# SAGE rounds of a graph network: GpSimd waits for the landing of two gathers in place of a clear between packets of two

## The reference, cut to what matters

```
def _sage_conv(x, src, dst, W_l, b_l, W_r, n_nodes):      # rounds 0 and 1
    agg = segment_sum(x[src], dst)                        # x[src]: the gather of this case
    mean = agg / maximum(cnt, 1.0)[:, None]
    out = mean @ W_l + b_l + x @ W_r
    return out / maximum(norm(out), 1e-12)
h = relu(_sage_conv(x, ...)); h = relu(_sage_conv(h, ...)); x = layernorm(x + h)

def sage_conv(h, W_l, W_r, bias):                         # rounds 2 to 5
    agg = segment_sum(h[src], dst) * inv_deg[:, None]
    return relu(agg @ W_l + h @ W_r + bias)
x = layernorm(x + h)                                      # after round 5
```

## Time and profile before

| | us |
|---|---|
| median of 3 runs | 14431.09 |
| lowest, highest | 14413.74, 14431.66 |
| the profiled execution's own time | 14447.17 |
| its span, first to last instruction | 14445.4 |
| PE busy | 9623.8 (67%) |
| DVE busy | 8218.2 (57%) |
| GpSimd busy | 5322.8 (37%) |
| ACT busy | 4574.6 (32%) |

### The profile page before, as it was taken

The page is one execution under the profiler, slowest core; times in us unless marked ns, Lnnn a source line. Parts: engine busy times, 40 slices in busy tenths (PEclk is TensorE's granted clock), DMA queues, the critical chain, the costliest instruction groups (busy, mean ns, idle before and its releaser), DMA issues. The chain is left out here.

```text
span 14445.4 us, 272192 instructions
## 1 busy us (share of the span) xinstructions
PE 9623.8 (67%) x51477; PEld 7110.9 (49%) x51673; DVE 8218.2 (57%) x25011; ACT 4574.6 (32%) x9542; POOL 5322.8 (37%) x6651
## 2 busy tenths in 40 slices
PE   2765567766666777777787777544544477777765
PEld 1112157755555666666666666333333244444444
DVE  4776567767774222222223555688888644444467
ACT  0000012235553222222222444455555422222257
POOL 0554543322222333333333333333333255555510
PEclk9887778877888988888988888666666678787776
DMA  9300046655555665665665666433333333333368
GB/s 324 116 3 1 1 136 195 194 160 180 181 180 165 186 186 180 186 184 176 184 188 175 208 209 210 137 123 122 116 122 122 114 95 98 99 98 94 96 193 270
DMA packets 2090713, 2169.75 MB, mean 150 GB/s; under 512 B 312033, under 2 KB 1419234, under 8 KB 2077614
## 3 DMA queue, kind: packets, MB, share of 16 engines
q1 hardware_dynamic: 1343046, 1025.71, 23.7%
q10 hardware_dynamic: 584524, 871.96, 17.5%
q0 software_dynamic: 163072, 271.31, 7.5%
HBM read 1407.48 MB, written 826.93 MB: 155 GB/s over the span
## 5 line engine op out<-in xcount | busy, mean ns | idle before, releaser
L778 POOL DMA_INDIRECT gath<-node_a,g_idx x1176 | 1130.4, 961 | 2606.5 <-PE edge_bank L980 1825.4
L1120 PE MATMUL o_bank<-keep,gsrc_t 128*128 (+1 forms) x9408 | 1475.6, 307 | 841.4 <-DMA keep<-rank_rows 810.3
L1844 DVE TENSOR_TENSOR gsrc_t<-node_no,keep 128x512 f32<-128x512 f32 x1176 | 807.9, 693 | 2125.9 <-PE o_bank L1120 1567.6
L1120 PEld LDWEIGHTS o_bank<-keep,gsrc_t 128*128 128x128 f32 x9408 | 1328.3, 218 | 958.4 <-issue 956.7
L1108 PE MATMUL o_bank<-w_r,h_t 128*128 128x128 f32 x9408 | 1744.2, 342 | 0.0
L1108 PEld LDWEIGHTS o_bank<-w_r,h_t 128*128 128x128 f32 x9408 | 1477.0, 239 | 340.5 <-issue 340.5
L787 POOL DMA_INDIRECT agg<-y_rows,s_idx x784 | 867.4, 1106 | 1445.5 <-DVE s_idx L1811 1082.1
L778 POOL DMA_INDIRECT gath<-node_x,g_idx x784 | 782.4, 998 | 1572.4 <-PE edge_bank L1032 589.5
L778 POOL DMA_INDIRECT gath<-node_b,g_idx x784 | 800.1, 1020 | 1016.4 <-PE edge_bank L980 461.2
L753 POOL DMA_INDIRECT rec_dram<-rec_rows,place_idx x784 | 761.1, 971 | 1093.8 <-DVE rec_rows L1760 857.3
L1295 ACT ACTIVATE h_t<-ht_bank 128x512 f32<-128x512 f32 x1176 | 688.3, 594 | 1345.3 <-PE ht_bank L1098 933.7
(11 more groups left out here) (388 smaller groups left out, 19355.0 us busy)
## 6 DMA issues: line engine op xcount, KB each, us to landing
keep<-rank_rows SPq DMA_DIRECT2D x4704, 64.0 KB
node_a<-h_out ACTq DMA_DIRECT2D x784, 256.0 KB
rank_rows<-y_rows SPq DMA_DIRECT2D x588, 256.0 KB
h_in<-node_a SPq DMA_DIRECT2D x396, 256.0 KB
node_x<-h_out ACTq DMA_DIRECT2D x394, 256.0 KB
node_b<-h_out ACTq DMA_DIRECT2D x394, 256.0 KB
agg<-zeros ACTq DMA_DIRECT2D x98, 1024.0 KB
agg_in<-agg SPq DMA_DIRECT2D x392, 256.0 KB
```

Of the source, the lines that this page charges most:

```text
L778: pool.indirect_dma_start(gath[q][:, k, :], None, h_of, bass.IndirectOffsetOnAxis(g_idx[q][:, k:k + 1], 0)).then_inc(gathered[q], 16)
L1120: last = pe.matmul(o_bank[s][:, j * P:(j + 1) * P], hot_node[s][:, j, :], ranks_at(s, u, j), start=False, stop=j == RPP - 1, skip_group_ch ...
L1844: dve.tensor_tensor(hot_node[s], node_no[:].unsqueeze(1).to_broadcast([P, RPP, P]), of.unsqueeze(2).to_broadcast([P, RPP, P]), ALU.is_equa ...
```

## The change

In the SAGE rounds, behind each two gathers, GpSimd waits until `gathered[q]` shows that these two have landed: the target less 32 behind the first two of a block, the full target behind the last two. The clears and the waits for them go from these rounds, and `pauses` no longer counts them. The first two blocks of a round, and the GAT and TR rounds, stay as they are.

```
-            GATHER_PAUSES = 4 * (PAIRS - 1)
...
-                pauses += GATHER_PAUSES if kind == SAGE else PAUSES
+                pauses += PAUSES if kind in STAGGERED else 0
...
-                def gathers_by_two(q, n, first, r=r):
+                def gathers_by_two(q, n, r=r):
                     pool.wait_ge(gt_ready[q], gt_ready.at(r, n - 1))
                     pool.wait_ge(gidx_ready[q], gidx_ready.at(r, n))
                     pool.sem_inc(pool_turn, 1)
                     for half in range(2):
                         gathers(q, of=range(2 * half, 2 * half + 2))
-                        pause(first + half)
+                        pool.wait_ge(gathered[q], gathered.at(r, n) - 32 * (1 - half))
                         pool.sem_inc(pool_turn, 1)
...
-                    gathers_by_two(q, 2, first_pause + 2 * q)
+                    gathers_by_two(q, 2)
...
-                        gathers_by_two(q, i + 3, i * 4 + (first_pause + 4 + 2 * q))
+                        gathers_by_two(q, i + 3)
```

## The result

The changed kernel takes 14530.91 us (median of 4 runs, 14520.95 to 14533.52) where the kernel before takes 14422.42 (median of 4 runs, 14407.16 to 14431.66). The ratio is 1.0075, with an interval of 1.0058 to 1.0092: 108 us slower. The forecast was 14605, the range 14480 to 14930.

What follows compares the result with a forecast made beforehand. SP's chain of landings was taken to bound rounds 2 to 4, the gather loop the heads. Terms of +84, +30, +45, +5 and +10 sum to +174 us: 14621 profiled, 14605 on the median, range 14480 to 14930.

Steps and rivals of the forecast that it cites:

- heads, 12 pairs: First two throttled pairs of six rounds: gather loop 20.0 us against 13.0, nothing covers it, +84 us.
- round 0: Its 45 middle pairs: loop of 22.0 us against a period of 21.66, plus uneven pairs, +30 us.
- short pairs and middles of rounds 2 to 4: Short pairs behind the heads +5 us a round; middles, loop just under the period, +10 each.
- rounds 1 and 5: Middles with 29.19 and 25.04 us a pair: longer loop hidden, but for some 5 us.
- scatter, ends of rounds: Gathers that now and then take longer than 0.95 us, and scattered landings: +10 us.
- L: Time from the end of the second gather instruction to its landing as seen: 2.0 us in heads, 2.5 in middles.
- B: Length of a pair's gather loop on GpSimd, 12 + 4L: 20.0 us in heads, 22.0 in middles.
- The long landing: Rival: landings of 3.0 us in the middles make the loop 24.0 us and the bound, about +440 us; chance 0.25.
- SP's chain: Rounds 2 to 4: SP's rank loads, their landing and row writes set the period, 22.36 us in one pair.
- uneven pairs and uneven landings use that up at times: +10 each: Middles of rounds 2 to 4: up to 4 us of cover for late turns is sometimes used up, +30 us together.
- Faster transfers on SP's chain: Rival: fewer gathers in flight speed rank loads in rounds 2 to 4; 14355 us at 1.2 a pair; chance 0.09.
- Hidden anyway: Rival: landings of 1.6 to 1.9 us throughout and 0.5 us a pair gained, 14431 give or take 25; chance 0.06.

Runs made afterwards that it cites:

- e2: Changed kernel with landing waits only in the first two throttled pairs of each SAGE round, clears from there on: 14460.83 us against 14369.61 for the kernel before.
- e1: Changed kernel with the clears kept in the first two throttled pairs of each SAGE round, landing waits behind them: 14451.13 us against 14369.61 for the kernel before.
- e6: Kernel before with a 128x2048 clear instead of 128x8 in every SAGE pause, no landing waited for: 14580.75 us against 14469.89.
- e4: Kernel before with landing waits in the middles of rounds 2 to 5 alone, clears in rounds 0, 1 and all heads: 14344.33 us against 14369.61.
- e3: Kernel before with neither clears nor landing waits in the SAGE rounds, eight gathers in a row: 15866.57 us against 14369.61.
- e10: Kernel before with a short clear and wait after each gather in place of each two in the SAGE rounds: 14343.43 us against 14451.64.
- e7: Kernel before with one short clear and wait after each four gathers in place of each two: 15648.92 us against 14469.89.
- e8: Changed kernel with one landing wait after each four gathers in place of each two: 15032.45 us against 14469.89 for the kernel before.
- e12: Kernel before with short clears after each gather in SAGE middles, each gather and scatter in GAT, each two in TR: 14086.84 us against 14479.32.

## Why the prediction was right, and where its sum was not

The direction and the range held, and so did the mechanism in its main part: the gather loop gets longer, it is the path in the heads, and it becomes the bound of rounds 2 to 4 at about their old period. The sum is 66 us too high, term by term:

| term | forecast | trace |
|---|---|---|
| heads, 12 pairs | +84 | +70.6 |
| round 0 | +30 | +47.7 |
| short pairs and middles of rounds 2 to 4 | +45 | -16.5 |
| rounds 1 and 5 | +5 | +37.5 and -25.4 |
| scatter, ends of rounds | +10 | -5.4 |
| sum | +174 | +108.5 |

The heads are the one large term that came out by its own mechanism. Behind them the forecast has +90 and the trace +37.9, which is +85.2 in rounds 0 and 1 less 47.3 elsewhere: that the rest lies near the forecast at all is owed to terms with opposite signs and not to the sum's working.

**Heads.** The step was right and L mis-sized: 1.5 to 1.7 us for most of the gaps where 2.0 was taken, so a head pair is 18.6 to 19.6 us and not 20.0. e2 has the same price with nothing else changed: the heads +75, the SAGE part +73, the time +91. But e1 shows that the heads' price isn't simply added: with the heads cured the middles took most of it back. Whether middles really run longer behind a short head, and why, wasn't found.

**L in the middle.** 2.5 was taken and 2.1 to 2.5 measured (gaps of 2.9 to 3.3 us), so that B is 22.14 us in round 2 where the forecast had 22.0. The eighth gather of a middle pair ends 17.7 to 19.2 us after the first starts (the means of the six rounds), nearly as said. The long landing, the rival with a chance of 0.25, isn't there: no round sits at 24 us except for those that had more before. Two of its numbers don't follow from their rows. The loads in the head added 0.92 to 1.09 us to a landing (2.69 against 1.77 and 1.60), not 0.69, which is the distance from the chosen 2.0. And 3.32 bounded one landing, not all: the longest gap of a middle, 5.7 us, leaves 4.9.

The Trainium skill, "DMA: Bandwidth & Descriptors", section "Anatomy of one DMA — SWDGE (gpsimd) path", has 2.0 us fixed and the bytes over 436 GB/s, an estimate of 2.15 us for such a gather. The traces lie on both sides of it, 1.53 in a quiet head pair and up to 2.5 on average in the middles, so it is a fair first figure but not one to set a 1% decision by. Counted from the start of a gather instruction, which takes 0.95 us itself, the landing comes after 2.5 us or so even in a quiet head. The HBM latency at high load that the Trainium skill gives on the same page, section "Latency and other measured facts", 2 us where the average is 0.2, would have made 3.4 by the prediction's estimate, and no round's mean comes near that.

**Round 0.** The sign is right and the mechanism holds in part: the loop of 22.0 was to pass a period of 21.66, and the pairs became 22.72. PE waits before its turn for 26.4 us where it was 4.5, mostly for gathers. But only 19 of the 45 pairs follow GpSimd's own last work, so the loop isn't the bound of the other 26, and what makes them longer wasn't found. The +30 counted uneven pairs on top of the loop; +47.7 was measured, and +54.8 in e1. e6 is no confirmation: its loop is too short to be the bound and DVE has 97 us more to do.

**Rounds 2 to 4.** The prediction left SP's chain as the bound, with the loop just under it; PE's waits show that the loop took its place (354 us of waits for gathers in rounds 2 and 3, where the earlier trace rows have 394.9 for rank rows). So "uneven pairs and uneven landings use that up at times: +10 each" has the path wrong: the loop replaced SP's chain, at 22.14 to 22.25 us, instead of lying beside it and adding to it at times, and the landings' scatter is in its mean already. The short pairs did grow, from 16.5 to 22.6 us in round 2, but in the changed kernel it was paid back behind them. The sizes say less than the path. These three middles are 16.5 us shorter in the changed kernel, but 24.0 and 19.2 longer in e1 and e4, which have the same landing waits there, and kernels that left them as they were differ by 40 us.

**Rounds 1 and 5.** "Hidden, but for some 5 us" is the step that failed, in both, with opposite signs. The cover was there (GpSimd's loop sets the period in none of round 1's 45 pairs and in two of round 5's), and the rounds changed all the same. Round 5 gained 25: four kernels with landing waits there have 1087.5 to 1105.0 us, long clears 1080.0 and 1091.2, short gaps of single gathers 1051.6 and 1040.8, against 1126.7 and 1133.0 for the old break. So wider spacing helps there, whichever way it is made; why it does stays open. Round 1 lost 37.5: 1351.2 and 1362.3 with landing waits, 1374.7 with long clears (and more work for DVE), 1313.7 to 1329.2 in six kernels with the old break. The trace has ACT and DVE waiting longer in it. Their groups in its middle (busy us, mean ns, idle us before them and what ended it), in the changed kernel and then in the one before:

```profile
L1328 ACT ACTIVATE zeros<-total 128x512 f32<-128x512 f32 x180 | 110.5, 630 | 474.9 <-DVE total L2049 460.6 <-issue 14.3
L1843 DVE TENSOR_TENSOR gsrc_t<-node_no,keep 128x512 f32<-128x512 f32 x180 | 124.7, 693 | 242.0 <-PE o_bank L1119 197.5 <-issue 44.0
```

```profile
L1329 ACT ACTIVATE zeros<-total 128x512 f32<-128x512 f32 x180 | 110.5, 629 | 429.9 <-DVE total L2050 278.5 <-issue 151.4
L1844 DVE TENSOR_TENSOR gsrc_t<-node_no,keep 128x512 f32<-128x512 f32 x180 | 124.6, 693 | 199.1 <-PE o_bank L1120 144.3 <-issue 53.6
```

ACT is idle 45 us longer before these, and DVE 43 us longer before its builds, which wait for PE's matmuls with the rank rows. DVE does the same 966 us of work in both, so it is late and not slower. PE is what takes longer: the same 1440 matmuls with rank rows are busy for 244.5 us where it was 218.7, and the 720 that turn node rows for 139.6 where it was 126.4, 39 us together, while the 1440 with W_r stay at 334 to 337. Two kernels with the old break (e2, e4) have 226 to 227 and 131 us for the two slower groups, e1 with landing waits 252 and 141. Why those two groups get slower when the gathers come later within their cover stays open; the granted clock in the stretch is 0.78 for 0.80, which goes with the longer waits and can't be told from their cause.

**The rivals.** Faster transfers on SP's chain: rounds 2 to 4 got 4.2, 4.7 and 7.6 us shorter behind their heads, which the prediction had named as a sign that it was wrong. It is within the scatter of a middle, and e1 and e4 have the opposite, so it doesn't speak for this rival; the clear gain was in round 5, for which the rival had claimed nothing, and the heads outweighed it. Hidden anyway: excluded by the heads, as argued. What the prediction didn't see at all is what the breaks are for. It took the clears as something from which "nothing but GpSimd gains"; e3 puts their worth at 1497 us, fourteen times the effect that was to be forecast. The wait for landings keeps that worth, which is why the change didn't cost more, and single gathers with short gaps (e10) did better than rows of two with either gap.

## What to carry to other kernels

Gathers that GpSimd sends four or eight in a row hold up what PE has finished for ACT and DVE, and probably scatters too, which were tried only together with gathers. Break such rows with something short (here a clear of 128x8 and the wait for it, about 1 us), after each one where GpSimd has room and after two where its loop is the path. Don't make the break a long clear, which also holds up DVE, or a wait for the landing: the gap is two to three times as long, and at the head of a round, where nothing else runs, all of it is paid. In a profile, look for waits without a releaser on the users of PE's results; they pointed at 230 us in a round that the change didn't touch. Breaks gave nothing in the GAT round, so try them stage by stage. And before reading one wait as grown, add up all that the engine idled before that instruction: the part put down to DVE grew by 182 us in round 1, the idle time by 45.

## What the runs showed of the hardware

- Rows of GpSimd's gathers delay what PE releases for DVE and ACT, and the large step lies between two and four: a short break after one, two and four gathers and none in eight (e10, before, e7, e3) stand at -108, 0, +1179 and +1497 us against before. A full landing after each four still leaves +563 (e8).
- The waits so held up end a set time after the last gather instruction of the row: mostly 1.7 to 1.9 us in e3, about 1.3 in e7 and 1.2 in e8.
- The gain isn't there in every stage (e12): breaks after each two gathers or scatters gave the TR round 230 us; breaks after each one gave the GAT round, where DVE is busy for 84% of the time, none.
- A gather instruction of 64 KB is on GpSimd for 0.95 us, follows another by 0.30, and is seen landed 1.5 to 1.7 us after its end in a quiet stretch and 2.1 to 2.5 on average in a loaded one; GpSimd needs another 0.8 to 1.0 to go on after the wait.
- A 128x2048 clear in f32 takes GpSimd 1.82 us where the 128x8 one takes 0.12. DVE's 128x128 build of a one-hot matrix, 0.34 us at the median, takes up to 2.6 us when it meets the long clear (e6), while its 128x512 build stays at 0.69.
